# Matmuls of constants on TensorE at positions 5 to 11 of each round, and in the last round between the sum and the transposes

## The chip, the cores and the metric

One core of one Trainium2 chip. The metric is the device time of one execution in microseconds; lower is better. Engines run their own instruction streams in order and meet through semaphores. PE is TensorE (PEld its weight loads), DVE VectorE, ACT ScalarE, POOL GpSimd, SP the queue that issues most DMAs. PE has a granted clock with two levels, 1.2 and 2.4 GHz, shown as 0.50 and 1.00.

## The reference

Eight graphs of 1024 nodes with 128 features. Per sample, first a max-aggregation over each node's first 25 neighbours, then a small feed-forward net whose weights depend on the node block:

```python
# gnn on layernorm(x)
vals, idx = jax.lax.top_k(jnp.where(A != 0, -arange(N), -inf), 25)
agg = jax.vmap(lambda x, i: x[i])(X, idx)   # absent neighbours: -inf
agg = agg.max(axis=2)                       # and 0 where degree <= 25
out = relu(concatenate([X, agg], -1) @ W + b)
x = x + out
# ffn on layernorm(x), route is one expert per 128 rows
h = relu(flat @ Wi.T + bi)
for l in range(2):
    h = relu(h @ Ws[l].T + bs[l] + (h @ Wr[l, route].T + br[l, route]) + h)
x = x + h @ Wo.T + bo
```

## The kernel before

The work is written as rounds s = 0 to 9 of 44 positions p = 0 to 43 (`positions()`); every engine walks the same list, and what it does at a position is written in tables at the head of the program. Round s does three things at once:

- `prepare(s, p)` reads sample s: masks of the adjacency on ACT, their transposes by DMA, prefix ranks on PE into the two banks `prep_f[0]` and `prep_f[1]` (positions `RANK_AT`: from 16 on in rounds after the first), copied by ACT into `rank` (semaphore `s_q`, two counts for each of 8 blocks).
- `slot(s-1, p)` is one step of the neighbour maximum of sample s-1. An engine (ACT, POOL or DVE, by `ACT_HOT`, `POOL_HOT`, `DVE_HOT`) has built a one-hot matrix a few positions ahead; PE multiplies the features by it (two parts, up to 896 columns, so four matmuls of 512 and 384 columns, or two for narrow slots, or twice as many for the group of two blocks) into one of two buffers `slot_ps`; DVE folds the buffer into `acc` by a maximum (line 988). PE starts slot n only when DVE has folded slot n-2 (`s_max`), its one-hot is there, and everything ahead of it in PE's own stream has been issued.
- `finish(s-2, p)` is the rest of sample s-2 in the banks `ffn_ps`: transposes of the features at p 0 and 1; the matmuls of the aggregation layer at p 2 to 5 (lines 811 and 812); on DVE the sum x1 at p 4 and 6 (line 1161) with statistics at p 5 and 7, and the norm at p 7 and 8 (lines 1005 to 1018, with a square root on ACT between, line 703); h0 on ACT at p 9 and 11 (line 612); its transposes on PE at p 12 and 13 (line 819), copied by ACT (line 618); the first dense layer at p 14 to 17 (line 826); the expert layers from p 19 and p 27 on (line 842); the output at 36 and 39 (line 852).

On PE the order at a position is `slot`, `finish`, `prepare`. In rounds 2 to 8 all three parts run. In round 1 PE also transposes the expert weights; round 9 has `finish` alone. `down` is a constant of 1024 float16 values for each partition, N down to 1, written once at the start. Nothing reads or writes `prep_f[0]` between the last rank copy of a round (p 38) and p 16 of the next; in round 9 it takes one small product at p 24.

Of the kernel before, what the change touches and what calls it, by code (L numbers as in the profile page):

```python
# [15 lines left out]
P = 128  # L16
# [47 lines left out]
def gnn_ffn_program(nc, x, adj, gnn_W, gnn_b, route_id, Wi, bi, Wr, br, Ws, bs, Wo, bo, out):  # L64
    B, N, C = x.shape
    IT = N // P
# [10 lines left out]
    BANK = 512  # L77
# [8 lines left out]
    CONSTS = 7  # L86
    assert HUBS == 1 and sorted(PLACES) == [(g, r) for g in range(NG) for r in range(1, CAPS[g][0] + 1)]
    assert NW == 34 and HC == 2 and L == 2 and all(w == TT for _, _, w in SLOTS[0:2])


# [28 lines left out]
                    12: [11], 13: [12], 14: [13], 15: [14], 16: [15], 17: [16], 19: [17], 20: [18], 21: [19],  # L119
                    22: [20], 23: [21], 24: [22], 25: [23], 26: [24]}  # L120
    FIRST_W_AT = 6
    OUT_AT = {36: 0, 39: 1}
    WEIGHTS_AT = [] + [NS + p for p in (
        0, 1, 2, 3, 4, 5, 6, 7, 9, 10, 11, 12, 14, 15, 16, 18, 19, 20, 22, 23, 24, 25,
# [14 lines left out]
    with ExitStack() as ctx:  # L139
        def sb(name, shape, dt=F32):  # L140
            return ctx.enter_context(nc.sbuf_tensor(name, shape, dt))
# [4 lines left out]
        def sem(name):  # L146
            return ctx.enter_context(nc.semaphore(name))
# [5 lines left out]
        down = sb("down", [P, N], F16)  # L153
# [74 lines left out]
        prep_f = [p[:, :].bitcast(F32) for p in prep_ps]  # L228
# [29 lines left out]
        s_q = sem("s_q")  # L258
# [62 lines left out]
        def positions():  # L321

            for s in range(B + 2):
                for p in range(NS):
                    yield s, p
# [22 lines left out]
        def weights_at(s, p, late):  # L348
            at_ = s * NS + p - late
            return [m for m in range(NW) if WEIGHTS_AT[m] == at_]  # L350
# [28 lines left out]
        def _(sp):  # L379
# [6 lines left out]
            def load_expert(k, i):  # L386

                e = sp.value_load(route[0:1, k * IT + i:k * IT + i + 1], min_val=0, max_val=NE)
                sp.dma_start(wst[:, i, :], folded[bass.ds(e, 1)].rearrange("a p w -> (a p) w")).then_inc(s_w[i], 16)
# [16 lines left out]
            for s, p in positions():  # L406
                k = s - 2
                if k == 0 and 0 <= p - FIRST_W_AT < IT:
                    if p == FIRST_W_AT:
                        sp.wait_ge(s_route, 1)  # L410
                        for i in range(NST):
                            sp.wait_ge(s_wstore[i], 16 * len(range(i, NW, NST)))
                        sp.wait_ge(s_bstore, 16)
                    load_expert(0, p - FIRST_W_AT)
                if s < B:
# [43 lines left out]
                if 0 <= k < B:  # L459
# [6 lines left out]
                    if p - 1 in LAYER_AT[1] and k + 1 < B:  # L466
                        i = LAYER_AT[1][p - 1]
                        sp.wait_ge(s_r[1], k * IT + i + 1)
                        load_expert(k + 1, i)
                    if p - 1 in OUT_AT:  # L470
                        g = OUT_AT[p - 1]
                        sp.wait_ge(s_y, 2 * k + g + 1)
# [279 lines left out]
        def _(pe):  # L752
            pe.wait_ge(s_const, CONSTS)

            def start_with_bias(bank, which):
                pe.matmul(bank, onesb[0:SPLITS, :], bias_rows[:, which].rearrange("p t c -> p (t c)"),
                          start=True, stop=False)

            def slot(b, p):
                n = b * NS + p  # L760
                g, r, wide = SLOTS[p]
                first, many = GROUPS[g]
                if p == 0:
                    pe.wait_ge(s_split, b + 1)
                if p in ACT_HOT:
                    pe.wait_ge(s_acthot, b * len(ACT_HOT) + ACT_HOT.index(p) + 1)
                elif p in POOL_HOT:
                    pe.wait_ge(s_poolhot, b * len(POOL_HOT) + POOL_HOT.index(p) + 1)
                else:
                    pe.wait_ge(s_onehot, b * len(DVE_HOT) + DVE_HOT.index(p) + 1)  # L770
                if n >= 2:
                    pe.wait_ge(s_max, n - 1)
                for j in range(many):
                    for part in range(PARTS):
                        for c0 in range(0, wide * P, BANK):
                            c1 = min(c0 + BANK, wide * P)
                            mm = pe.matmul(slot_ps[n % 2][:, c0:c1], xsplit[:, b % 2, part, first + j, :],  # L777
                                           onehot[:, UNIT[n] + j, c0:c1], start=(j == 0 and part == 0),
                                           stop=(j == many - 1 and part == PARTS - 1))
                mm.then_inc(s_slot, 1)  # L780

            def finish(k, p):
# [46 lines left out]
                for l in range(L):  # L829
                    if p in LAYER_AT[l]:  # L830
# [13 lines left out]
                        mm.then_inc(s_l[l], 1)  # L844
                if p in OUT_AT:
                    g = OUT_AT[p]
                    pe.wait_ge(s_r[1], k * IT + 7 + g)
# [8 lines left out]
            def prepare(s, p):  # L856
                if p in RANK_AT[s > 0]:
                    jt = RANK_AT[s > 0][p]
                    second = [f for f, many in GROUPS if many == 2 and f + 1 == jt]
                    for c in range(CHUNKS):  # L860
                        if jt == 0:
                            for i, many in enumerate(turns((s + 1) * TT)):
                                pe.wait_ge(s_turn[i], 16 * many)
                            if s > 0:
                                pe.wait_ge(s_q, 2 * IT * s - 1 + c)
                        else:
                            pe.wait_ge(s_q, 2 * IT * s + 2 * jt + c - 1)
                        cols = slice(c * CW, (c + 1) * CW)
                        mm = pe.matmul(prep_f[c][:, 0:CW], before[:, :], at[:, jt, cols],  # L869
                                       start=True, stop=not second)  # L870
                        if second:
                            mm = pe.matmul(prep_f[c][:, 0:CW], onesb[:, :], at[:, jt - 1, cols],
                                           start=False, stop=True)
                        mm.then_inc(s_rank, 1)
# [11 lines left out]
            for s, p in positions():  # L886
                if 1 <= s <= B:
                    if s == 1 and p == 0:
                        pe.wait_ge(s_biases, 1)
                    slot(s - 1, p)  # L890
                if 2 <= s:
                    finish(s - 2, p)
                if s < B:
                    prepare(s, p)
                if (s, p) == (B + 1, VERDICT_AT):
                    pe.wait_ge(s_above, 1)
                    pe.matmul(prep_f[0][0:1, 0:ROWS], above[:, 0:1], ident[0:ROWS, 0:ROWS], start=True,
                              stop=True).then_inc(s_overs, 1)
                for m in weights_at(s, p, 0):
                    if m < NIN:  # L900
                        pe.wait_ge(s_wfirst[m // 4], 16 * 4)
                    else:
                        pe.wait_ge(s_wload[m % NIN], 16 * (m // NIN))
                    if m >= 2:
                        pe.wait_ge(s_wfold, m - 1)
                    for kc in range(HC):
                        for hc in range(HC):
                            mm = pe.transpose(ffn_ps[m % 2][:, (kc * HC + hc) * P:(kc * HC + hc + 1) * P],  # L908
                                              w_in[m % NIN][:, hc, kc * P:(kc + 1) * P], ident[:, :])
                    mm.then_inc(s_wT, 1)  # L910
# [42 lines left out]
        def _(dve):  # L953
# [201 lines left out]
            def finish(k, p):  # L1155
# [9 lines left out]
                if p - 1 in SUM_AT:  # L1165
                    g = SUM_AT[p - 1]
                    dve.wait_ge(s_sum, 2 * k + g + 1)
                    for i in range(4 * g, 4 * g + 4):
                        dve.bn_stats(stats[:, 1, i, :], x1[:, i, :])
                if p - 1 in OUT_AT:  # L1170
                    g = OUT_AT[p - 1]
                    dve.wait_ge(s_o, 2 * k + g + 1)
# [119 lines left out]
```

## Time and profile before

| | us |
|---|---|
| median of 3 runs | 735.02 |
| lowest and highest | 734.71, 737.31 |
| the profiled execution | 736.18 |
| its span, first to last instruction | 734.5 |
| mean granted clock of PE in it | 0.926 |

| engine | busy us | share of the span | instructions |
|---|---|---|---|
| PE (matmuls) | 611.5 | 83% | 3496 |
| PEld (weight loads) | 502.9 | 68% | 3497 |
| DVE | 574.2 | 78% | 959 |
| ACT | 521.2 | 71% | 981 |
| POOL | 541.9 | 74% | 388 |

All engines are busy for two thirds to four fifths of the span, so a share says little about which one holds up the others at a given place. That is read from the rows: a timeline gives for one engine the start and duration of each group of like instructions and, in brackets, how long the engine was idle before it and what ended the idle time; the chain is followed back from the last instruction, at each step to what released it.

### The profile page before, as it was taken

What the parts mean: (1) busy time and instruction counts of PE and PEld (TensorE: products, weight loads), DVE (VectorE), ACT (ScalarE), POOL (GpSimd) and SP (SyncE); (2) the same over time, 40 slices, a digit from 0 to 9 for tenths busy, and PEclk for the clock granted to TensorE, in tenths of its full rate; (3) what the DMA queues carried; (4) which work ended last, traced back from release to release, by engine and by line L of the source; (5) the groups of instructions that cost most, each with busy time, mean ns of one, the idle gap of its engine ahead of it and who ended that gap; (6) DMA issues with size and microseconds to landing.
All of it is one profiled execution on the core that took longest, in us unless ns stands there. A gap on an engine that the chain in (4) does not pass through costs nothing.

```text
span 734.5 us, 11755 instructions
## 1 busy us (share of the span) xinstructions
PE 611.5 (83%) x3496; PEld 502.9 (68%) x3497; DVE 574.2 (78%) x959; ACT 521.2 (71%) x981; POOL 541.9 (74%) x388
## 2 busy tenths in 40 slices
PE   0466666679999799979997999899987999799686
PEld 0054545566987588858885888668875988588565
DVE  3766799878987898779987898789878987777740
ACT  5672455369977898779876987699769985478062
POOL 4577488497979987898878897989799878984000
PEclk9986798898999899979998999989998999799989
DMA  9999997479746965496638755785474543045222
GB/s 298 305 196 265 314 344 241 134 176 293 226 132 158 267 175 152 102 259 205 166 109 222 236 163 142 190 240 159 127 182 124 161 138 87 22 113 144 58 72 77
DMA packets 145171, 131.73 MB, mean 179 GB/s; under 512 B 72219, under 2 KB 112324, under 8 KB 145092
## 3 DMA queue, kind: packets, MB, share of 16 engines
q1 hardware_dynamic: 128124, 105.94, 53.5%
q0 software_dynamic: 7296, 15.74, 8.3%
q10 hardware_dynamic: 9680, 9.21, 4.5%
q8 instruction: 31, 0.51, 0.3%
q14 instruction: 40, 0.33, 0.1%
HBM read 98.20 MB, written 17.98 MB: 158 GB/s over the span
## 4 chain that ended last, share of the span: by engine, by line
PE 59%; DVE 22%; issue 5%; DVEq 4%; DMA 4%; ACT 4%; SPq 1%; ACTq 0%
PE slot_ps L777 28%; PE ffn_ps L842 11%; DVE acc L988 9%; PE ffn_ps L852 4%; PE ffn_ps L826 4%; PE prep_ps L869 3%; DMA at<-mask 2%; PE ffn_ps L811 2%; PE ffn_ps L792 2%; DVEq L1060 2%; DVE top L1047 2%; PE ffn_ps L812 2%; DMA adj_sb<-in_adj_dram 2%; DVE wst L1153 1%; DVE score L1049 1%
## 5 line engine op out<-in xcount | busy, mean ns | idle before, releaser
L777 PE MATMUL slot_ps<-onehot,xsplit 128*128 128x512 f32 (+3 forms) x1376 | 375.5, 401 | 51.1 <-DVE acc L988 44.4
L988 DVE TENSOR_TENSOR acc<-slot_ps,acc 128x896 f32<-128x896 f32 (+2 forms) x336 | 293.7, 884 | 77.3 <-PE slot_ps L777 74.5
L547 POOL TENSOR_SCALAR onehot<-rank,ranks 128x896 fp32r<-128x896 bf16 (+3 forms) x128 | 298.4, 2333 | 72.6 <-PE slot_ps L777 67.5
L777 PEld LDWEIGHTS slot_ps<-onehot,xsplit 128*128 128x128 f32 x1376 | 251.9, 204 | 105.7 <-issue 71.0
L535 POOL DMA_INDIRECT gath<-feature_table,idx x200 | 207.7, 1038 | 47.9 <-issue 42.6
L842 PE MATMUL ffn_ps<-hT,wst 128*128 128x128 f32 x1024 | 135.1, 277 | 0.0
L842 PEld LDWEIGHTS ffn_ps<-hT,wst 128*128 128x128 f32 x1024 | 129.0, 191 | 5.9 <-issue 0.8
L670 ACT ACTIVATE away<-rank,ranks 128x896 bf16<-128x896 bf16 (+4 forms) x136 | 107.9, 793 | 6.8 <-DVE wst L1153 6.4
L687 ACT ACTIVATE onehot<-away 128x896 fp32r<-128x896 bf16 (+4 forms) x136 | 96.3, 708 | 21.5 <-PE slot_ps L777 10.6
L629 ACT ACTIVATE hT<-ffn_ps,wst 128x128 f32<-128x128 f32 x256 | 81.1, 375 | 29.5 <-PE ffn_ps L842 27.3
L641 ACT ACTIVATE rank<-prep_ps 128x448 bf16<-128x448 f32 x128 | 63.0, 550 | 21.0 <-PE prep_ps L869 11.7
L714 ACT ACTIVATE mask<-adj_sb 128x1024 bf16<-128x1024 uint32 x56 | 58.0, 1047 | 25.8 <-DMA at<-mask 20.9
L681 ACT ACTIVATE onehot<-rank,ranks 128x896 fp32r<-128x896 bf16 (+1 forms) x48 | 56.0, 1167 | 22.1 <-PE slot_ps L777 21.3
L869 PE MATMUL prep_ps<-at,before 128*128 128x448 bf16 x128 | 39.9, 380 | 15.0 <-DMA at<-mask 12.3
L908 PE MATMUL ffn_ps<-ident,hT 128*128 128x128 f32 x136 | 26.5, 329 | 28.8 <-DVE wst L1153 25.7
L908 PEld LDWEIGHTS ffn_ps<-ident,hT 128*128 128x128 f32 x136 | 18.8, 169 | 38.8 <-issue 36.7
L1047 DVE MAX8 top<-score 128x8 f32<-128x1024 f32 x32 | 39.0, 1219 | 0.3
L975 DVE TENSOR_SCALAR onehot<-rank,ranks 128x1792 fp32r<-128x1792 bf16 (+2 forms) x40 | 38.5, 962 | 0.7 <-PE slot_ps L777 0.7
L826 PE MATMUL ffn_ps<-xnT,wiT 128*128 128x512 f32 x64 | 33.4, 611 | 0.5 <-ACT xnT L618 0.5
L852 PE MATMUL ffn_ps<-woT,hT 128*128 128x128 f32 x256 | 32.8, 281 | 0.0
L869 PEld LDWEIGHTS prep_ps<-at,before 128*128 128x128 bf16 x128 | 11.4, 99 | 30.9 <-DMA at<-mask 12.4
L852 PEld LDWEIGHTS ffn_ps<-woT,hT 128*128 128x128 f32 x256 | 29.8, 191 | 3.6 <-issue 3.6
(121 smaller groups left out, 586.3 us busy)
## 6 DMA issues: line engine op xcount, KB each, us to landing
wst<-folded_weights SPq DMA_DIRECT2D x128, 257.0 KB, 2.9
adj_sb<-in_adj_dram SPq DMA_DIRECT2D x64, 512.0 KB, 5.9
folded_weights<-wst ACTq DMA_DIRECT2D x34, 256.0 KB, 6.9
hT<-in_L_ffn_Wr_dram SPq DMA_DIRECT2D x26, 256.0 KB, 10.3
xs<-in_x_dram SPq DMA_DIRECT2D x8, 512.0 KB, 8.1
feature_table<-xn SPq DMA_DIRECT2D x8, 512.0 KB, 4.1
x<-in_x_dram SPq DMA_DIRECT2D x8, 512.0 KB, 4.3
out_dram<-h SPq DMA_DIRECT2D x16, 256.0 KB, 2.4
```

The source lines that it names most:

```text
L535: pool.indirect_dma_start(gath[:, j, :], None, tables[b], bass.IndirectOffsetOnAxis(ap=idx[:, b % 2, 0, j:j + 1], axis=0)).then_inc(signal ...
L547: pool.tensor_scalar(onehot[:, UNIT[n]:UNIT[n] + many, 0:wide * P], rank[:, b % 2, first:first + many, 0:wide * P], ranks[:, r - 1:r], Non ...
L629: ins = act.activation(hT[:, 1 - l, j, i, :], ffn_ps[(i + 1) % 2][:, j * P:(j + 1) * P], ACT.Relu, bias=wst[:, i, HC * HID + j:HC * HID + ...
L641: act.activation(rank[:, s % 2, jt, c * CW:(c + 1) * CW], prep_f[c][:, 0:CW], ACT.Copy, bias=float(NONE)).then_inc(s_q, 1)
L670: act.activation(away[:, i % AWAYS, 0:wide * P], rank[:, b % 2, first, 0:wide * P], ACT.Square, bias=ranks[:, r - 1:r], scale=-1.0).then_i ...
L687: act.activation(onehot[:, UNIT[n], 0:wide * P], away[:, i % AWAYS, 0:wide * P], ACT.Relu, bias=1.0, scale=-1.0).then_inc(s_acthot, 1)
L777: mm = pe.matmul(slot_ps[n % 2][:, c0:c1], xsplit[:, b % 2, part, first + j, :], onehot[:, UNIT[n] + j, c0:c1], start=(j == 0 and part == ...
L826: pe.matmul(ffn_ps[1 - j][:, :], wiT[:, j * P:(j + 1) * P], h0T[:, 4 * g:4 * g + 4, :].rearrange("p t c -> p (t c)"), start=True, stop=Tru ...
L842: mm = pe.matmul(ffn_ps[(i + 1) % 2][:, j * P:(j + 1) * P], wst[:, i, c0:c0 + P], hT[:, l, kc, i, :], start=(kc == 0), stop=(kc == HC - 1))
L852: mm = pe.matmul(o, hT[:, 0, kc, i, :], woT[:, kc, :], start=False, stop=(i % 4 == 3 and kc == HC - 1))
L869: mm = pe.matmul(prep_f[c][:, 0:CW], before[:, :], at[:, jt, cols], start=True, stop=not second)
L988: dve.tensor_tensor(acc[:, p % 2, 0:cols], slot_ps[n % 2][:, 0:cols], acc[:, p % 2, 0:cols], ALU.max).then_inc(s_max, 1)
```

## The change

A new function on PE multiplies `down[:, 0:128]` (as weights) by `down[:, 0:512]` into the bank `prep_f[0]`. Nobody reads the results. In rounds 2 to 8 it runs ahead of the slot at positions 5 to 11 (25 matmuls a round), in round 9 at positions 6 to 11 after `finish` (24). At its first position of a round it waits until all rank copies of the round before are done.

```diff
+    BUSY_AT = {5: 2, 6: 4, 7: 5, 8: 5, 9: 4, 10: 3, 11: 2}
+    BUSY_AT_END = {6: 4, 7: 4, 8: 4, 9: 4, 10: 4, 11: 4}
...
+            def keep_busy(s, p):
+
+                where = BUSY_AT if s < B + 1 else BUSY_AT_END
+                if p == min(where):
+                    pe.wait_ge(s_q, 2 * IT * min(s, B))
+                for _ in range(where.get(p, 0)):
+                    pe.matmul(prep_f[0][:, 0:BANK], down[:, 0:P], down[:, 0:BANK], start=True, stop=True)
...
                 if 1 <= s <= B:
                     if s == 1 and p == 0:
                         pe.wait_ge(s_biases, 1)
+                    if s >= 2:
+                        keep_busy(s, p)
                     slot(s - 1, p)
                 if 2 <= s:
                     finish(s - 2, p)
+                if s == B + 1:
+                    keep_busy(s, p)
                 if s < B:
                     prepare(s, p)
```

## Rows read from the trace of the kernel before

**Rows 1.** Page, 40 slices of 18.4 us: granted TensorE clock, tenths
```profile
PEclk9986798898999899979998999989998999799989
```

**Rows 2.** Page, chain that ended last: share of the span
```profile
PE 59%; DVE 22%; issue 5%; DVEq 4%; DMA 4%; ACT 4%; SPq 1%; ACTq 0%
```

**Rows 3.** Windows: PE, PEld, DVE, ACT, POOL busy (x instructions), clock, DMA, GB/s
```profile
240.00:244.00 4.00, 1.21 (x5) 0.84 (x6) 3.50 (x11) 2.34 (x5) 3.75 (x4) 0.91 1.06 348
244.00:248.00 4.00, 2.06 (x9) 1.80 (x9) 4.00 (x5) 4.00 (x9) 3.80 (x3) 0.50 0.77 124
248.00:252.00 4.00, 4.00 (x18) 3.25 (x16) 1.27 (x3) 4.00 (x9) 3.79 (x3) 0.74 1.00 225
...
696.00:700.00 4.00, 0.15 (x1) 0.15 (x2) 3.11 (x10) 2.06 (x6) 0.00 (x0) 0.65 0.00 0
```

**Rows 4.** Timeline, PE, round 3: start us, us, what [idle before <-releaser]
```profile
233.56 1.06 PE L777 MATMUL slot_ps<-onehot,xsplit 128*128 128x512 f32 x4
...
235.27 1.68 PE L777 MATMUL slot_ps<-onehot,xsplit 128*128 128x384 f32 x6
237.13 1.04 PE L777 MATMUL slot_ps<-onehot,xsplit 128*128 128x512 f32 x4 [0.18 <-DVE acc L988]
...
243.85 0.66 PE L777 MATMUL slot_ps<-onehot,xsplit 128*128 128x128 f32 x2 [0.83 <-DVE acc L988]
246.45 0.98 PE L777 MATMUL slot_ps<-onehot,xsplit 128*128 128x384 f32 x2 [1.95 <-DVE acc L988]
```

**Rows 5.** Timeline, DVE, the same stretch
```profile
234.66 1.09 DVE L988 TENSOR_TENSOR acc<-slot_ps,acc 128x896 f32<-128x896 f32 x1 [1.33 <-PE slot_ps L777]
...
237.50 1.08 DVE L988 TENSOR_TENSOR acc<-slot_ps,acc 128x896 f32<-128x896 f32 x1
...
240.74 1.08 DVE L988 TENSOR_TENSOR acc<-slot_ps,acc 128x896 f32<-128x896 f32 x1
...
250.83 1.09 DVE L988 TENSOR_TENSOR acc<-slot_ps,acc 128x896 f32<-128x896 f32 x1 [2.73 <-PE slot_ps L777]
```

**Rows 6.** Chain in order of time (start us, us, what), 212 to 218 us
```profile
214.75 0.19 PE prep_ps L872
```

**Rows 7.** Chain, 310 to 342 us, round 4
```profile
325.13 2.99 PE slot_ps L777 x8
...
336.66 1.64 PE slot_ps L777 x8
```

**Rows 8.** Copy of the transposed h0 on ACT, and PE behind it: rounds 3, 5, 2
```profile
250.43 0.57 ACT L618 ACTIVATE xnT<-ffn_ps 128x512 f32<-128x512 f32 x1
...
251.58 0.86 PE ffn_ps L826 x2
...
405.74 0.58 ACT L618 ACTIVATE xnT<-ffn_ps 128x512 f32<-128x512 f32 x1
...
407.40 0.86 PE ffn_ps L826 x2
...
173.10 0.49 ACT xnT L618
...
173.63 1.13 PE ffn_ps L826 x2
```

**Rows 9.** Chain, 633 to 650 us, round 8
```profile
633.74 0.98 PE slot_ps L777 x2
...
639.73 0.86 PE ffn_ps L826 x2
```

**Rows 10.** Chain, 690 to 735 us, last round
```profile
693.43 0.24 PE ffn_ps L812 x2
...
701.39 1.11 PE ffn_ps L819 x4
702.50 4.46 PE ffn_ps L826 x8
706.97 5.90 PE ffn_ps L842 x48
```

## The prediction

> **What bounds the kernel now.** I read the page first, then the chain of work that ended last, then one round (the third, 223.7 to 301.4 us; round s does the slots of sample s-1 and the feed-forward part of sample s-2) engine by engine. The page's clock line [rows 1] shows the half clock once in each round. The chain [rows 2] runs through PE for 59% and DVE for 22%, and alternates between them inside a round. The windows [rows 3] show one fall: PE is busy 1.21 of 4 us, and the clock, 0.91 there, is 0.50 in the next window and 0.74 in the one after. In full speed and half speed that is 0.7 + 4.0 + 2.1 = 6.8 us at 1.2 GHz instead of 2.4. The same is seen in all rounds 2 to 8 and once in the tail (0.65, then 0.50).
>
> The question is what PE holds up there. At positions 5 to 11 it holds up nothing late in the stretch: it waits for DVE, which folds slots, sums x1 and works out the norms. PE's row at 246.45 (slot 12) has 1.95 us of idle before it and the one at 237.13 (slot 8) only 0.18 [rows 4]. But the stretch begins the other way round: at 234.66 DVE has sat idle 1.33 us for slot 5 [rows 5], and is then busy without a gap until it waits 2.73 us for slot 13 at 250.83. So two places have no slack: PE before slot 5, and DVE from its fold of slot 5 to its fold of slot 10. Cold PE work lies on the path only from slot 12 on.
>
> **The filling: its price.** A filling matmul is 512 columns. The nearest row is 448 columns in 0.19 us at full clock, with another weight matrix loaded in between [rows 6]; 512 columns make 0.213 us, weight loads hidden. Each round from 2 to 8 gets 2+4+5+5+4+3+2 = 25 of them, 5.3 us, issued ahead of the slot of their position, and a matmul waiting behind them can't pass.
>
> Position by position in round 3. Slot 5 starts at 233.56 [rows 4]; 2 fillings make it 233.99. Slot 6 starts 1.71 later in PE's row (235.27); with 4 more it starts at 233.99 + 1.71 + 0.85 = 236.55. Its two matmuls of 384 columns take 0.35, 5 more fillings 1.07, so slot 7 starts at 237.97. A slot of four matmuls is ready 1.06 + 0.04 after its start (233.56 to 234.66, rows 4 and 5): slot 7 at 239.07. DVE began that fold at 237.50 [rows 5]. So 11 fillings, 2.35 us, delay DVE by **1.57 us**; 0.8 is covered by DVE's work between folds 5 and 7. From there on the cover is enough: slot 8 would be ready at 239.90 - 0.04 + 1.10 = 240.96, while DVE, late by 1.57, comes to it at 240.74 + 1.57 = 242.31; slots 9 to 11 have still more. The last 14 fillings cost nothing, the first 11 cost 1.57.
>
> Rounds 2 and 4 to 8 show the same rows at the same distances, so I count 7 x 1.57 = 11.0 us. Behind the delayed fold 7 stand x1's statistics, the square root on ACT, the norm, ACT's normalising of h0, and with that the whole feed-forward part. The wait that the change adds, for all rank copies of the round before, costs nothing: the one-hot of slot 2 (group 6, the last) already needs them all. Upper bound of the price: all 5.3 us a round, if nothing covered any; lower bound 0, if DVE had slack that the rows don't show.
>
> **What the full clock gives.** From slot 12 to slot 14 at half clock PE needs 0.98 + 0.85 + 2.99 + 0.7 + 0.35; the double slot of 2.99 us takes 1.64 at full clock [rows 7], and the whole stretch 3.2 instead of 5.1 to 6.2 us. It doesn't all come back, since the first dense matmul of position 14 needs ACT's copy of the transposed h0, and ACT has been busy without a gap since the norm. That copy ends at 251.00 in round 3 where PE began at 251.58, at 406.32 against 407.40 in round 5 [rows 8]: 0.58 and 1.08 us to gain. By the same pair of rows round 4 has 0.8 and round 7 0.5. In rounds 2 and 6 the chain already runs through that copy (173.59, then PE at 173.63): nothing. Round 8 has no mask and no xn on ACT; there PE is the bound, from 633.74 to 639.73 [rows 9], and 5.99 becomes 3.22: 2.8 us. Sum 5.8 us, at most, if the clock stays up.
>
> The tail: 24 fillings, 5.1 us, begin when the sum's matmuls end at 693.67 and end at 698.8. The transposes start at 699.85; no cost, 1.0 us of margin. At full clock the second transposes end at 702.0 instead of 702.50, and the dense stage, 4.46 us at half clock [rows 10], is bound by PE and ACT in turn: copy to 702.6, then four times about 0.65 of ACT with PE between, so that the layers start at 704.7 instead of 706.97. Gain **2.2 us**.
>
> With the clock held everywhere: +11.0 - 5.8 - 2.2 = **+3.0 us**.
>
> **Does the clock stay up?** The fillings end at position 11, ahead of slot 11; the largest idle time left is after it, 2.3 us ahead of slot 12 (the 1.95 of 246.45 [rows 4] and what the half clock of slot 11 hides of it now). In the new order PE runs from 243.5 to 244.8, again for 0.1 at 245.4 and then from 248.0: 4 us with about 1.3 busy, much like the 1.21 before which it fell [rows 3]. So in part of the rounds it should fall after all, only later, beside slots 12 to 16, where PE's work counts. ACT's copy covers 1.3 us of that. A fall of 6.8 us would cost about 1.2 in rounds 2 to 7 and take away the 2.8 of round 8: none to 9.7 us. I take three rounds at 0.7: **+2.1 us**.
>
> **The sum**: 3.0 + 2.1 = +5.1 us. The profiled execution took 736.18 us (span 734.5, 1.7 around it), 1.2 over the median of 735.02; it makes 741.3 of the first, and **740.1** of the median.
>
> A filling costs what a row shows, yet one rule sets another price. The Trainium skill, TensorE: Matmul & The Clock Gate, "Back-to-back issue gap", gives a sustained spacing of about 131 ns for 512 columns in a stream of load and matmul pairs. The row of 448 columns at 0.19 us speaks against it. By that rule 11 fillings would be an estimated 1.4 us, the delay 0.7, and the time about 733.
>
> **Rivals.**
> 1. *Held everywhere.* As above without a late fall: 738.0. For it: PE is busy in most of every stretch. Against it: the unfilled gap ahead of slot 12.
> 2. *The change doesn't do what it says*: the fillings don't keep the clock up, or it falls in nearly every round in the late gap and in the tail. The delay of 11.0 stays, the gains don't: 746. It decides once rounds 2 to 8 still hold a half-clock stretch each beside work that PE's end depends on. Were the clock half in the tail's fillings too, the last of them would end at 700.3, 0.5 us too late.
> 3. *Faster: the fillings are hidden.* If folds 5 to 7 have slack (a dependency that I place wrongly) or DVE makes up the delay in its later waits, only gains are left: 735.0 - 5.8 - 2.2 = 727. For it: DVE is idle 1.33 and 2.73 us in the round. Against it: both idle times end on PE, one ahead of the fillings and one after them, and between them the chain has DVE alone. It decides if fold 7 follows fold 5 after less than 3.3 us (2.84 now, 3.98 by the working above).
> 4. *Cheaper fillings*, at about 0.13 us each by the same working: delay 0.7 a round, 4.6 in all, 735.0 + 4.6 - 8.0 + 1.4 of late falls = 733. Against it: the 448-column row.
>
> **Chances.** Forecast 0.43 (738.7 to 744), held everywhere 0.22 (735 to 739), no clock 0.13, hidden 0.15, cheaper 0.07. The range leaves out the hidden case (0.15) and the far end of the no-clock one: 730 to 746.5, from below the cheaper case to just above the delay without any gain. A measurement of this kernel tells 0.5%, 3.7 us, from no change: faster (under 731.3) is the hidden case and a little of the cheaper one, 0.17; within 0.5% are held everywhere, most of cheaper and the low end of the forecast, 0.34; slower (over 738.7) 0.49.
>
> **What would show it.** In the new trace: fillings 0.21 us apart; slot 7's fold about 4.0 us after slot 5's instead of 2.84, and no idle time of DVE for slot 13 beyond 1 us; ACT's copy of h0 followed at once by PE; the clock line without a fall at positions 7 to 11, and with one, in some rounds, at positions 12 to 16; the last layers starting 2 us sooner after the last sum. The forecast is wrong if fold 7 isn't late, if the clock stretches are as before, or if PE waits for the copy less than I say because ACT's order leaves it a gap.

## The result, and the profile after

| | us |
|---|---|
| before, median of 4 | 736.12 (734.71 to 737.31) |
| with the change, median of 4 | 744.46 (741.39 to 745.93) |
| ratio | 1.0109, 95% interval 1.0066 to 1.0151 |
| with the change, measured again beside the experiments | 744.44, ratio 1.0117, interval 1.0092 to 1.0142 |
| the profiled execution, its span, its mean clock | 743.35, 741.5, 0.968 |

The change makes the kernel slower by 1.1 to 1.2%, 8.3 to 8.5 us between the medians, though it does to the clock what it says: 0.968 on average instead of 0.926. From the page, the granted clock in 40 slices and the chain by engine:

```profile
PEclk9997898999999999999999999999999999999999
...
PE 61%; DVE 19%; issue 5%; DVEq 4%; ACT 4%; DMA 3%; SPq 3%; ACTq 0%
```

Against [rows 1] the dips of rounds 2 to 8 are nearly gone. A digit 9 stands for 0.90 and more, so a short dip may hide in it. Windows over rounds 2 to 8 tell more (length; busy time of PE, PEld, DVE, ACT, POOL; granted clock; DMA share; GB/s), first of before, then of the change:

```profile
146.81:686.24 539.43, 494.14 (x2913) 415.62 (x2912) 451.73 (x711) 426.96 (x819) 448.06 (x284) 0.95 0.62 167
144.73:692.89 548.16, 515.37 (x3087) 421.91 (x3087) 456.33 (x711) 426.90 (x819) 447.17 (x284) 0.99 0.62 164
```

58.0 us of rounds 2 to 8 were at half clock before, 13.7 are with the change: one stretch of 3.4 us in each of rounds 2 to 5. Against [rows 2] PE's share of the chain has grown from 59% to 61%. Round 3 starts 0.5 us sooner here than in the profile of before; what counts below are distances inside the round. First the same windows in round 3 and the tail, the answer to [rows 3]:

```profile
240.00:244.00 4.00, 3.35 (x17) 1.75 (x16) 3.40 (x14) 1.67 (x3) 2.65 (x3) 1.00 1.09 357
244.00:248.00 4.00, 1.59 (x8) 0.92 (x8) 3.93 (x7) 3.60 (x7) 3.57 (x2) 0.95 0.37 75
248.00:252.00 4.00, 4.00 (x18) 3.63 (x17) 1.37 (x3) 4.00 (x10) 3.79 (x3) 0.62 0.93 186
...
708.00:712.00 4.00, 3.96 (x9) 1.92 (x10) 3.47 (x11) 1.75 (x3) 0.00 (x0) 0.57 0.00 0
```

PE is busy 3.35 us in the window in which it had 1.21, and at full clock. The fall comes one window later, after the 1.59 of 244 to 248, and beside PE's dense work. The last row is the same in the tail: 0.57 where the first dense stage runs. PE's timeline (start, duration, what, idle time before it), the answer to [rows 4]:

```profile
233.16 0.59 PE L767 MATMUL prep_ps<-down 128*128 128x512 f16 x2
233.41 1.16 PE L787 MATMUL slot_ps<-onehot,xsplit 128*128 128x512 f32 x4
...
235.97 0.69 PE L787 MATMUL slot_ps<-onehot,xsplit 128*128 128x384 f32 x2
236.50 1.25 PE L767 MATMUL prep_ps<-down 128*128 128x512 f16 x5
237.41 1.17 PE L787 MATMUL slot_ps<-onehot,xsplit 128*128 128x512 f32 x4
...
244.91 0.41 PE L787 MATMUL slot_ps<-onehot,xsplit 128*128 128x128 f32 x2 [0.38 <-DVE acc L1002]
247.36 0.77 PE L787 MATMUL slot_ps<-onehot,xsplit 128*128 128x384 f32 x2 [2.04 <-DVE acc L1002]
```

Line 767 is the filling. PE has no idle time ahead of the first of them, so the added wait for the rank copies costs nothing. Slot 5 comes at 233.41 behind its 2, slot 7 at 237.41 behind its 5. Slot 11 is at 244.91, and the gap ahead of slot 12 is 2.04 us. DVE's folds of slots 5, 7, 8 and 13, the answer to [rows 5]:

```profile
234.60 1.09 DVE L1002 TENSOR_TENSOR acc<-slot_ps,acc 128x896 f32<-128x896 f32 x1 [1.75 <-PE slot_ps L787]
...
238.61 1.09 DVE L1002 TENSOR_TENSOR acc<-slot_ps,acc 128x896 f32<-128x896 f32 x1 [0.76 <-PE slot_ps L787]
...
241.80 1.08 DVE L1002 TENSOR_TENSOR acc<-slot_ps,acc 128x896 f32<-128x896 f32 x1
...
251.64 1.09 DVE L1002 TENSOR_TENSOR acc<-slot_ps,acc 128x896 f32<-128x896 f32 x1 [2.63 <-PE slot_ps L787]
```

From fold 5 to fold 7 it is 4.01 us, where it was 2.84, and DVE now waits 1.75 us for slot 5 and 0.76 for slot 7. ACT's copy of the transposed h0 in round 3 (timeline) and PE's first dense matmul (chain of waits), the answer to [rows 8]:

```profile
251.50 0.58 ACT L620 ACTIVATE xnT<-ffn_ps 128x512 f32<-128x512 f32 x1
...
252.39 0.86 PE ffn_ps L836 x2
```

The copy ends at 252.08 and PE starts at 252.39. From fold 5 that is 17.79 us, against 16.92 before, and 0.42 more lies in the wait for slot 5: 1.3 in all, of the 1.6 that fold 7 is late. The dense stage and the layers of the last round in the chain, the answer to [rows 10]:

```profile
708.85 5.17 PE ffn_ps L836 x8
714.02 5.87 PE ffn_ps L852 x48
```

5.17 us instead of 4.46: the clock fell inside it (708.4 to 711.8).

### The profile page after: what moved, and what is told of

It is laid out like the page before. It is cut to its first block, busy times and chain, and to the rows that moved or that the text cites. A ratio compares the mean times of both kernels' runs of the same rounds, so it can differ in the third digit from the quotient of the medians.

```text
span 741.5 us, 12153 instructions
## 1 busy us (share of the span) xinstructions
PE 632.7 (85%) x3695; PEld 506.6 (68%) x3696; DVE 579.9 (78%) x959; ACT 520.8 (70%) x981; POOL 541.6 (73%) x388
## 4 chain that ended last, share of the span: by engine, by line
PE 61%; DVE 19%; issue 5%; DVEq 4%; ACT 4%; DMA 3%; SPq 3%; ACTq 0%
PE slot_ps L787 28%; PE ffn_ps L852 11%; DVE acc L1002 7%; PE ffn_ps L862 4%; PE ffn_ps L836 4%; PE prep_ps L879 3%; PE ffn_ps L821 2%; PE prep_ps L767 2%; DMA at<-mask 2%; PE ffn_ps L822 2%; PE ffn_ps L802 2%; DVEq L1074 2%; SPq L423 2%; DVE onehot L989 2%; DVE top L1061 2%
## 5 line engine op out<-in xcount | busy, mean ns | idle before, releaser
L787 PE MATMUL slot_ps<-onehot,xsplit 128*128 128x512 f32 (+3 forms) x1376 | 363.8, 390 | 37.5 <-DVE acc L1002 30.3
L787 PEld LDWEIGHTS slot_ps<-onehot,xsplit 128*128 128x128 f32 x1376 | 243.5, 196 | 90.0 <-issue 45.9
L922 PE MATMUL ffn_ps<-ident,hT 128*128 128x128 f32 x136 | 24.7, 312 | 32.9 <-DVE wst L1167 26.5
L767 PE MATMUL prep_ps<-down 128*128 128x512 f16 x199 | 51.5, 381 | 0.0
L989 DVE TENSOR_SCALAR onehot<-rank,ranks 128x1792 fp32r<-128x1792 bf16 (+2 forms) x40 | 40.5, 1012 | 0.6 <-issue 0.6
L705 ACT ACTIVATE std<-mv 128x16 f32<-128x16 f32 (+1 forms) x10 | 2.1, 214 | 51.2 <-DVE mv L1027 45.6
```

The costliest lines, as they stand in the source:

```text
L767: pe.matmul(prep_f[0][:, 0:BANK], down[:, 0:P], down[:, 0:BANK], start=True, stop=True)
```

## Experiments

To see the rounds apart from chance I add up, from PE's timeline, the time from the first matmul of the feature transposes in round 2 to the same one in round 9 (146.81 to 686.24 before). Each figure is of one profiled execution; e3_tail and e6_xn, which have no fillings in these rounds, differ from before by 0.6 and 0.0. What is ahead of round 2 (144 to 147 us) varies more, by 2.3 us between e5_gap_xn and e5_again, and what is behind round 8 by up to 1.9 between two executions of the same kernel, with the moments at which the clock falls there.

| kernel | what it has | whole, against before [95% interval] | rounds 2 to 8, us | then to the end, us |
|---|---|---|---|---|
| before | | 1 | 539.43 | 48.22 |
| the change | fillings at 5 to 11 and in the tail | 1.0109 [1.0066, 1.0151] | 548.16 | 48.65 |
| after_again | the same | 1.0117 [1.0092, 1.0142] | 549.20 | 47.05 |
| e2_early | only ahead of slots 5 to 7 | 1.0154 [1.0130, 1.0178] | 551.19 | 49.06 |
| e1_late | only ahead of slots 8 to 11, and tail | 1.0000 [0.9984, 1.0016] | 540.47 | 50.46 |
| e3_tail | only tail | 0.9971 [0.9957, 0.9985] | 540.04 | 48.92 |
| e8_double | twice as many ahead of 5 to 7 | 1.0309 [1.0277, 1.0341] | 563.05 | 47.19 |
| e7_after_p12 | the change and 7 ahead of slot 12 | 1.0107 [1.0078, 1.0136] | 548.07 | 48.68 |
| e4_gap | only where PE waits, slots 8 to 12, and tail | 0.9953 [0.9933, 0.9973] | 537.15 | 49.19 |
| e4_again | the same | 0.9967 [0.9946, 0.9989] | 537.15 | 47.28 |
| e6_xn | no filling; one pair of xn later on ACT | 1.0015 [0.9997, 1.0032] | 539.46 | 48.19 |
| e5_gap_xn | e4_gap and e6_xn | 0.9932 [0.9909, 0.9955] | 534.99 | 47.49 |
| e5_again | the same | 0.9915 [0.9890, 0.9940] | 535.17 | 47.60 |
| e9_seven | e5_gap_xn and 3 ahead of slot 7 | 0.9927 [0.9901, 0.9952] | 535.20 | 47.69 |

### Which fillings cost: e2_early and e1_late

Theory A is the prediction's: the 11 fillings ahead of slots 5 to 7 stand in front of work for which DVE waits. Theory B puts the loss on the later fall of the clock.

```diff
-    BUSY_AT = {5: 2, 6: 4, 7: 5, 8: 5, 9: 4, 10: 3, 11: 2}
-    BUSY_AT_END = {6: 4, 7: 4, 8: 4, 9: 4, 10: 4, 11: 4}
+    BUSY_AT = {5: 2, 6: 4, 7: 5}
+    BUSY_AT_END = {}
```

> Only the 11 fillings ahead of slots 5, 6 and 7 (2, 4, 5) in rounds 2 to 8, none behind them and none in the last round. Theory A: fold 7 follows fold 5 after 4.0 us, 1.57 us more in each of 7 rounds, with little given back, since the clock falls about where it fell before: +9 to +11.5 us, 744 to 748 us. Theory B: the clock falls as before, early, so no loss: within 2 us of the kernel before.

```diff
-    BUSY_AT = {5: 2, 6: 4, 7: 5, 8: 5, 9: 4, 10: 3, 11: 2}
+    BUSY_AT = {8: 5, 9: 4, 10: 3, 11: 2}
```

> Fillings at positions 8 to 11 only in rounds 2 to 8 (5, 4, 3, 2), the last round as in the change; the result is unchanged. Theory A (the 11 fillings ahead of slots 5, 6 and 7 stand in front of work that DVE waits for): DVE's fold of slot 7 follows that of slot 5 after 2.84 us again, the 11.0 us of delay are gone, and what is left is the gain of a clock that falls later: 728 to 735 us, faster than before or equal. Theory B (the loss comes from the late fall of the clock beside slots 12 to 16, not from where the fillings stand): the late falls stay, and so does the loss: 741 to 746 us.

Measured: e2_early 747.64 us against 735.86 (1.54% slower by the ratio, 11.3 us; the medians are 11.8 apart, and so are rounds 2 to 8); e1_late 735.85, a ratio of 1. The folds of slots 5 and 7 on DVE in round 3 of e2_early:

```profile
235.54 1.09 DVE L1002 TENSOR_TENSOR acc<-slot_ps,acc 128x896 f32<-128x896 f32 x1 [1.75 <-PE slot_ps L787]
...
239.55 1.09 DVE L1002 TENSOR_TENSOR acc<-slot_ps,acc 128x896 f32<-128x896 f32 x1 [0.76 <-PE slot_ps L787]
```

and of e1_late:

```profile
234.62 1.09 DVE L1002 TENSOR_TENSOR acc<-slot_ps,acc 128x896 f32<-128x896 f32 x1 [1.33 <-PE slot_ps L787]
...
237.46 1.08 DVE L1002 TENSOR_TENSOR acc<-slot_ps,acc 128x896 f32<-128x896 f32 x1
```

4.01 us with the early fillings alone, 2.84 with the late ones alone. The delay is the early fillings' and they cost 11.3 to 11.8 us. Theory B falls for the greater part: the early fillings alone, at a clock over rounds 2 to 8 like that of before (0.95), lose more than the whole change. That e1_late gains nothing is a miss of the range 728 to 735, by 0.9 us. Its clock still falls beside slots 12 to 16 in five of the seven rounds, for longest in round 6 (window, then the one of a fall in the last round ahead of the fillings there):

```profile
478.90:485.80 6.90, 6.24 (x21) 5.69 (x22) 3.69 (x6) 6.08 (x13) 6.39 (x5) 0.51 0.88 217
690.60:694.00 3.40, 3.40 (x17) 3.00 (x15) 0.17 (x1) 0.00 (x0) 0.00 (x0) 0.50 0.03 7
```

The two rounds without a fall take as long as in e4_gap, below; the five with one are 3.3 us longer together, 2.0 of it in round 6. So without the delay in front of them such falls do cost.

### Doubling the cost, and the size of the cover: e8_double and e9_seven

```diff
+    BUSY_AT = {5: 4, 6: 8, 7: 10, 8: 5, 9: 4, 10: 3, 11: 2}
```

> The change with twice as many fillings ahead of slots 5, 6 and 7 (4, 8, 10), the rest as in the change. Theory A: the cover of 0.8 us is used up by the first 11, so the other 11 of 0.213 us each delay DVE's fold of slot 7 in full: it follows fold 5 after 5.93 us (4.01 and the nine added fillings behind slot 5, 1.92; the two ahead of slot 5 move both), 2.35 us more in each of 7 rounds, 16.4 us more than the change, 761 us. Theory B: no more than the change, 744 us.

```diff
+    BUSY_AT = {7: 3, 8: 4, 9: 4, 10: 4, 11: 4, 12: 7}
```

> e5_gap_xn and 3 fillings (0.64 us) ahead of slot 7. In the kernel before, PE waits 0.26 us ahead of slot 7 and that slot is ready 0.51 us before DVE folds it: a cover of 0.77 us. Theory A: 3 fillings fit, fold 7 follows fold 5 after 2.84 us still, the time is that of e5_gap_xn, 730 to 731 us. If any filling ahead of slots 5 to 7 is paid in full: 0.64 us in 7 rounds, 735 us.

(e9_seven has e5_gap_xn, below, as its base.) Folds of slots 5 and 7 in round 3, first of e8_double:

```profile
237.82 1.09 DVE L1002 TENSOR_TENSOR acc<-slot_ps,acc 128x896 f32<-128x896 f32 x1 [2.20 <-PE slot_ps L787]
...
243.77 1.09 DVE L1002 TENSOR_TENSOR acc<-slot_ps,acc 128x896 f32<-128x896 f32 x1 [1.83 <-PE slot_ps L787]
```

then of e9_seven:

```profile
233.29 1.09 DVE L1002 TENSOR_TENSOR acc<-slot_ps,acc 128x896 f32<-128x896 f32 x1 [1.33 <-PE slot_ps L787]
...
236.13 1.08 DVE L1002 TENSOR_TENSOR acc<-slot_ps,acc 128x896 f32<-128x896 f32 x1
```

e8_double: 5.95 us between the folds, 759.14 us in all, 14.7 more than the change where 16.4 were expected; in the rounds 14.9 more than the change. So each filling beyond the cover is paid nearly in full: 0.19 of its 0.21 us. e9_seven: 2.84 us, and 730.46 against 729.79 of e5_again beside it, within their intervals. Three fillings fit into the cover of 0.77 us. The price is a matter of the place: free up to the cover, then about 0.2 us each.

### What the late fall costs: e7_after_p12

```diff
+    BUSY_AT = {5: 2, 6: 4, 7: 5, 8: 5, 9: 4, 10: 3, 11: 2, 12: 7}
```

> The change and 7 more fillings ahead of slot 12 (1.5 us in the last gap of 1.7 to 2.0 us), so that the clock should not fall beside slots 12 to 16. Theory A: the delay of 11.0 us stays, and what is gained against the change is the price of the late falls: 1 to 4 us less than the change, 739 to 742 us, still slower than before. Theory B (the late falls are the whole loss): no loss left, 730 to 736 us.

The window over its rounds 2 to 8, then slot 12 and the first dense matmul of round 3 on PE:

```profile
144.53:692.60 548.07, 521.17 (x3137) 420.86 (x3136) 459.93 (x711) 426.95 (x819) 445.76 (x284) 1.00 0.62 164
...
246.66 0.59 PE L787 MATMUL slot_ps<-onehot,xsplit 128*128 128x384 f32 x2 [0.51 <-DVE acc L1002]
...
251.44 1.13 PE L836 MATMUL ffn_ps<-xnT,wiT 128*128 128x512 f32 x2 [1.18 <-ACT xnT L620]
```

The clock holds through rounds 2 to 8 (1.00, and no stretch at half), and it is worth next to nothing: 743.01 us beside 744.44 of the change, with intervals that overlap and above the 739 to 742 expected, and in the rounds 548.07 us beside 548.16 and 549.20. PE, at full clock, has slot 14 done and sits idle 1.18 us for ACT's copy. The late falls of the change cost between 0 and 1.1 us, not 2.1; the loss is the delay, and the held clock doesn't pay for it. Theory B falls altogether.

### Fillings only in the gaps: e4_gap and e4_again

```diff
+    BUSY_AT = {8: 4, 9: 4, 10: 4, 11: 4, 12: 7}
+    BUSY_AT_END = {6: 4, 7: 4, 8: 4, 9: 4, 10: 4, 11: 7, 12: 3, 14: 1, 15: 1, 16: 1}
```

> Fillings only where PE waits for DVE: 4 each ahead of slots 8 to 11 and 7 ahead of slot 12 in rounds 2 to 8; in the last round 3 more ahead of the first transposes, 3 between the two groups of transposes and one behind each of the first three dense matmuls. Theory A with the clock held throughout: no delay, the 5.8 us of rounds 3, 4, 5, 7, 8 and the 2.2 of the tail back: 727 to 731 us. If the gain behind slot 12 is limited by ACT more than estimated, or the 7 fillings ahead of slot 12 are too many in rounds 2, 4, 5, 6, 8 (gap of 1.8 us there, 1.5 us of fillings): 731 to 735. Theory B: as the first, since no late fall is left: below 732.

> e4_gap again, beside e5_again on the same chip. 732 to 733 us, as before.

Measured 732.80 and 733.04 us, 0.3 to 0.5% less than before: faster, but short of 727 to 731. The window over rounds 2 to 8, then slot 12 and the first dense matmul in round 3:

```profile
145.05:682.20 537.15, 507.95 (x3073) 413.69 (x3073) 459.97 (x711) 426.76 (x819) 444.54 (x284) 1.00 0.63 168
...
244.71 0.59 PE L787 MATMUL slot_ps<-onehot,xsplit 128*128 128x384 f32 x2 [0.66 <-DVE acc L1002]
...
249.33 1.13 PE L836 MATMUL ffn_ps<-xnT,wiT 128*128 128x512 f32 x2 [1.16 <-ACT xnT L620]
```

The gap ahead of slot 12 still leaves 0.66 us, so the 7 are not too many, and the clock holds. In the rounds it gives 2.3 us; 5.8 had been reckoned. PE is idle 1.16 us for ACT's copy (249.28). e7_after_p12 and e4_gap, both at full clock in all seven rounds, also give the cleanest price of the early fillings: 548.07 against 537.15, 10.9 us.

### Is it ACT's queue: e5_gap_xn, e5_again, e6_xn

```diff
     XN_AT = [[3, 4, 5, 6],
-             [11, 13, 14, 16]]
+             [12, 13, 14, 16]]
```

At position 12 ACT does its copy first and xn after it, so 0.77 us leave the queue ahead of the copy. e5_gap_xn has this and the fillings of e4_gap, e6_xn this alone.

> The fillings of e4_gap, and ACT's first pair of xn normalisations moved from position 11 to 12, behind its copy of the transposed h0 (0.77 us of ACT taken from ahead of that copy; nothing left out). In the profile of e4_gap PE sat idle 1.16 us for that copy in round 3. Theory C (at full clock ACT's queue ahead of the copy is the bound, which is why the held clock gives so little): PE's first dense matmul comes 0.77 us sooner in rounds 2 to 7, up to 4.6 us less than e4_gap, 728 to 730 us. If something behind the copy takes the place of the wait (DVE's folds): no difference to e4_gap, 732 to 733 us.

> The kernel before without any filling, with only the move of xn from position 11 to 12. Theory C: at half clock ACT's copy was the bound in rounds 2 and 6 alone (there up to 0.77 us each), elsewhere PE's cold work: 0 to 1.5 us less than before, 734 to 736 us. If the move is worth the same with and without fillings, 4.6 us less: 731 us.

> e5_gap_xn again, beside e4_again. Theory C (ACT's queue ahead of the copy limits what the held clock gives): 1 to 3 us less than e4_again, 730 to 731 us. If the move of xn does nothing: the same as e4_again.

Without fillings the move is worth nothing (736.26 us, 1.0015, interval 0.9997 to 1.0032; rounds 539.46 against 539.43). With them it takes 2.0 to 2.2 us off the rounds, and side by side 729.79 us (e5_again) against 733.04 (e4_again). So ACT's queue is the bound ahead of the dense stage once the clock holds, and PE's half clock was it before. It gives 2 us and not 4.6 (730.43 for e5_gap_xn, just above its 728 to 730). PE's first dense matmul in round 3 of e5_gap_xn:

```profile
248.81 1.12 PE L836 MATMUL ffn_ps<-xnT,wiT 128*128 128x512 f32 x2 [0.39 <-DVE acc L1002]
```

The idle time is 0.39 us instead of 1.16 (ACT's copy and DVE's fold of slot 13 both end at 248.76, so the gap tells no more which of the two is the bound). The second dense matmul then waits for the second copy, which the move has put behind the xn. At 0.7 to 0.85% under before, e5_gap_xn is the fastest version tried.

### The tail: e3_tail and after_again

```diff
+    BUSY_AT = {}
+    BUSY_AT_END = {6: 4, 7: 4, 8: 4, 9: 4, 10: 4, 11: 4}
```

> Only the 24 fillings of the last round. They end about 1 us before the transposes start, so they cost nothing. If the clock stays up to the layers: 2.2 us less than before. If it falls in the first dense stage, as in the profile of the change (layers 13.9 us after the sum's matmuls instead of 13.3): 0 to 0.6 us more than before. Theory A and B agree here; the run tells what part of the change's time lies in the tail.

> The change as it is, again, beside the other kernels of this call, for a finer interval. From the first measurement 741 to 746 us; if the parts add up (early fillings +11.3 us, last round -2.1, the late fillings between 0 and +2): 745 us.

e3_tail alone measured 734.20 us, ratio 0.9971: 2.1 us less, interval 1.1 to 3.2. Its profiled execution shows no such gain: the clock fell inside the dense stage, and the part behind round 8 is 0.7 us longer than before. after_again met the case in which it holds; the dense stage and the layers in its chain:

```profile
709.80 3.72 PE ffn_ps L836 x8
...
713.53 5.90 PE ffn_ps L852 x48
```

3.72 us instead of 4.46 [rows 10], and from the second transposes (709.15) to the layers 4.38 instead of 5.58: 1.2 us gained, not 2.2. So the tail gives from +0.7 to -1.2 us, as the clock happens to fall or not behind the fillings; in e1_late it fell ahead of them too, and the part behind round 8 is 2.2 us longer. That the runs of e3_tail came out lower than its tail explains is left open; the stretch ahead of round 2 varies by as much.

## Why the prediction was right, point by point

- *Direction and size.* +5.1 us was forecast, +8.3 and +8.5 measured, inside the range of 730 to 746.5. The cause of the loss was right; that the number came out no further off is in part luck. 744.4 lies above the 738.7 to 744 that the forecast's own case was given, and nearer to rival 2's 746 than to 740.1. Rival 2's condition isn't met, though: in the profiled execution rounds 6 to 8 hold no half-clock stretch, and the clock over the rounds is 0.99. Its price comes close because the gains, which it puts at nothing, are small for other reasons, below. Rival 1 is out as well: with the clock held in all seven rounds e7_after_p12 takes 743.01, not 738.0.
- *The price of a filling.* Right to 1%. PE in the last round (timeline):

```profile
700.15 5.34 PE L767 MATMUL prep_ps<-down 128*128 128x512 f16 x24
706.50 0.66 PE L829 MATMUL ffn_ps<-ident,h 128*128 128x128 f32 x4 [1.01 <-ACT h L614]
```

24 fillings take 5.34 us and 2 take 0.61 (round 3, at 243.93): 0.215 us for each one more. The sustained 131 ns of the Trainium skill (TensorE: Matmul & The Clock Gate, "Back-to-back issue gap") isn't met: with it the 24 would end 2 us sooner. The rival of cheaper fillings is out.
- *The delay.* Right to a few hundredths: folds 5 and 7 were said to be 3.98 us apart and are 4.01; the delay of 11.0 us was measured as 10.9 (e7_after_p12 less e4_gap) and 11.3 to 11.8 (e2_early), the cover of 0.8 us is there (e9_seven), and beyond it each filling costs its own time (e8_double). The rival of hidden fillings is out.
- *The late fall.* It comes where it was said, behind the unfilled gap ahead of slot 12, in rounds 2 to 5 (after_again: 2 to 6), where three rounds were forecast. Its price was set too high, 2.1 us for 0 to 1.1: ACT's copy hides most of it. One sign failed with it: DVE was to wait no more than 1 us for slot 13, and in round 3 it waits 2.63.
- *The gain of the full clock in the rounds: the term that was mis-sized.* 5.8 us were taken off. With the clock held and no delay the rounds give 2.3 (e4_gap); with the clock held and the delay they lose 8.6 (e7_after_p12), so 2.4 of the 11.0 come back. Rounds 3, 4, 5 and 7 were to give 3.0 us, what ACT's copy leaves, and give 1.7. Part of this is a misreading: the row 251.58 [rows 8] is from the chain, where a step starts once the step before it has ended, and the timeline has the same matmul of before sooner:

```profile
251.42 1.02 PE L826 MATMUL ffn_ps<-xnT,wiT 128*128 128x512 f32 x2
```

That is 16.76 us after fold 5, and 16.43 in e4_gap (249.33, fold 5 at 232.90): 0.33 us sooner and not 0.58. Round 8 was to give 2.8 and gives 0.5 (73.40 to 72.94 us). The stretch from slot 12 to the first dense matmul does shrink there as reckoned, to 3.3 us, but it begins 1.1 us later in the round. Both DVE and POOL matter there: DVE's one-hot of slot 13, POOL's beside it, the reduction behind slot 14 and POOL's one-hot beside that, in round 8 of e4_gap (timelines), then the same four of before:

```profile
627.83 2.30 DVE L989 TENSOR_SCALAR onehot<-rank,ranks 128x1792 fp32r<-128x1792 bf16 x1
628.15 2.77 POOL L549 TENSOR_SCALAR onehot<-rank,ranks 128x896 fp32r<-128x896 bf16 x1
635.45 2.29 DVE L1089 TENSOR_TENSOR gath<-gath 128x768 f32<-128x768 f32 x1
635.89 2.56 POOL L549 TENSOR_SCALAR onehot<-rank,ranks 128x896 fp32r<-128x896 bf16 x1
...
631.41 1.19 DVE L975 TENSOR_SCALAR onehot<-rank,ranks 128x1792 fp32r<-128x1792 bf16 x1
631.86 3.14 POOL L547 TENSOR_SCALAR onehot<-rank,ranks 128x896 fp32r<-128x896 bf16 x1
640.24 1.58 DVE L1075 TENSOR_TENSOR gath<-gath 128x768 f32<-128x768 f32 x1
639.98 2.56 POOL L547 TENSOR_SCALAR onehot<-rank,ranks 128x896 fp32r<-128x896 bf16 x1
```

DVE's two take 1.8 us longer than before. The first pair is the same two operations in both kernels: before, DVE's is short and POOL's long, in e4_gap it is the other way round, and so in rounds 4 and 6 (1.14 us before, 2.19 in e4_gap). What decides which of the two is the long one, no run shows. The reduction ends 1.84 or 1.85 us after POOL's one-hot began in both, and that one-hot begins only 0.5 us sooner in the round than before, as much as the round gains. So in round 8 the rows point to POOL and DVE together as the next bound; no experiment moved them. I had worked out PE's time at full clock there and not asked what DVE and POOL do then.

- *The tail.* Costless as said, with 1.01 us of margin (706.50 above), but its gain is 1.2 us at best instead of 2.2: from the end of the second copy to the layers it is 3.1 us in after_again, and I had taken 2.1 (ACT's copies there start 0.86 to 1.05 us after one another, where I had 0.65; four steps of 0.65 would have made 2.6 in any case). In the profiled execution of the change the clock fell in it and cost 0.4. The second copy in after_again (timeline of ACT; the layers start at 713.53):

```profile
709.84 0.60 ACT L620 ACTIVATE xnT<-ffn_ps 128x512 f32<-128x512 f32 x1 [0.26 <-PE ffn_ps L829]
```

- *The sum in the runs' numbers:* +10.9 (early fillings), -2.3 (full clock in the rounds), +0.1 to +1.1 (late falls), -1.2 to +0.4 (tail): 7.5 to 10.1, measured 8.3 and 8.5. The forecast's 5.1 is under it because its gains were 8.0 and the real ones at most 3.5; the late falls, set too high, made up for part.

## What to carry to other kernels

Filling matmuls that hold up TensorE's clock paid here only in time in which TensorE waits anyway, and in an in-order queue that is judged slot by slot: by how long the consumer (here DVE) can still do without the slot behind them. The limit at a place is TensorE's own idle time there plus the distance from the slot's readiness to its use (0.26 + 0.51 us ahead of slot 7, where three fillings were free). Before one pays anything for the clock, one should ask who is next in the queue at full clock; here it was ScalarE, less than 1 us behind, and a reordering there, worthless alone, doubled the gain; in the last round of slots the rows point to GpSimd and VectorE.

## What the runs showed of the hardware

- The clock falls though PE has worked in between: in round 3 after 4 us with 1.21 busy before, and with 1.59 busy with the change, where the longest single gap ahead of the fall is 2.04 us. In e4_gap, whose gaps ahead of slot 12 are 0.5 to 1.3 us, it stays up through rounds 2 to 8.
- Half clock costs little where another engine is the bound: 58.0 us of it in rounds 2 to 8 were worth 2.3 us (before against e4_gap).
- An operation of DVE can take more than twice its time beside one of POOL, and it depends on when POOL's begins. POOL's one-hot and DVE's maximum of gathered rows (128 x 768 elements), each from its timeline, in round 8 of the change, then in round 4 of before:

```profile
646.60 2.55 POOL L549 TENSOR_SCALAR onehot<-rank,ranks 128x896 fp32r<-128x896 bf16 x1
...
646.14 2.30 DVE L1089 TENSOR_TENSOR gath<-gath 128x768 f32<-128x768 f32 x1
...
329.55 2.55 POOL L547 TENSOR_SCALAR onehot<-rank,ranks 128x896 fp32r<-128x896 bf16 x1
330.75 0.95 DVE L1075 TENSOR_TENSOR gath<-gath 128x768 f32<-128x768 f32 x1
```

In round 4 the maximum lies wholly inside POOL's one-hot and still takes 0.95 us. Where it was begun from 0.46 us ahead to 0.9 us behind the start of such a one-hot, it ended 1.83 to 1.85 us after that start: 1.84 above, 1.84 in round 8 of before (640.24, 1.58 us), 1.85 in e4_gap (635.45, 2.29 us). So by these rows it is held only in about the first 0.9 us of POOL's operation. The Trainium skill says in GPSIMD Engine Reference, "Specifications", that GpSimd's SBUF interfaces are shared with VectorE, with contention for DVE instructions that have two SBUF inputs; this one has two, and the trace agrees in that it slows down, 2.30 us for 0.95, though not for all of POOL's operation. That this is the whole cause of the longer one-hots (one input, 1.14 to 2.30 us in the same kernels) wasn't tried.
